# A four-pass FFN beside attention on one core: fillers for TensorE in the setup, the product kept in PSUM, and the score maximum ahead of the residual

## The chip, the cores and the metric

One of the eight cores of a Trainium2 chip runs the whole program. The metric is the device time of one launch in microseconds (us); smaller is better. Engines: TensorE (PE) multiplies into PSUM; VectorE (DVE), ScalarE (ACT) and GpSimd (POOL) do the rest; SyncE (SP) starts the DMAs. PEld is TensorE's weight load, which overlaps its matmuls.

## The reference, cut to what matters

```python
x = x + xattn(layernorm(x), fside, ctx, ctx)      # B=16 batches of 256 tokens, D=256
x = x + ffn(layernorm(x))
# xattn: 16 heads of 16; q = ln(x)@Wq+bq; keys and values = [fside@Wk+bk ; ctx] (512 rows)
#        softmax(q k^T / 4) v, then @Wp + bp
# ffn:   8 experts, dense; for each expert e (w_gate, w_up: 256x1024; w_down: 1024x256)
h   = silu(t @ w_gate[e]) * (t @ w_up[e])
out = sum_e (h @ w_down[e]) * cw[:, e]    # cw: product of two softmaxes, normalised
```

## The kernel before, in words

Every large operand is split into a high part, rounded for the fast fp32 matmul, and the rest, the low part; a product takes three passes (high*high, high*low, low*high). ACT makes the high part by a copy that rounds, DVE or POOL the low part by a subtraction.

The order of all work is written out by hand, as one loop for each engine over turns b = -2..18 of 32 steps. In turn b the attention of batch b runs, one step for each of its 32 score tiles. `ITEMS` gives each step at most one small job of PE with a reader behind it (`do_misc`: transposes, projections; "kT" and "qq" bring keys and queries into `KTs` and `QTs`). From step 19 of turn 2 (`START` = 83) one FFN step f goes with each step, 512 of them: a group of two batches takes 64 of them (8 experts by 8 slices of 128 hidden columns). Attention ends with turn 15; some 85 FFN steps follow without it.

In one joint step PE issues, in this order: `gate(f+1)` (6 matmuls of 512 columns into `ps_g`), `up(f+1)` (6 into `ps_u`), `down(f)` (6 into `ps_o`), every fourth step the 32 small value matmuls ("AV", L735 and L737), the job of the step, one score matmul S (L753) for eight steps ahead, and one T (L763), the transposed score tile that ACT exponentiates into `Pt`. `ps_g` and `ps_u` are the second banks of `ps_s` and `ps_t`, so once the FFN runs S has a single bank and waits until DVE has taken the maximum of the S before (`wait_scores_read`). Before `START` S has two banks, and there is no FFN work.

The FFN step on the other engines, by line:

- ACT `tanh_of` L777: `hf` = tanh(`ps_g`/2), then DVE `gate_of` L937: `hf` = (`hf`+1)*`ps_g`, then DVE `hidden_of` L944: `hf` = `hf`*`ps_u` (the product), then ACT `high_of` L782: `h_hi` from `hf`, then DVE `low_of` L949: `h_lo` = `hf` - `h_hi`, then PE `down`. There is one `hf`, so the next tanh waits for `low_of` (`hl_done`), and `up(f)` waits for the product f-1 (`hf_done`).
- DVE's queue in a step: `gate_of`, `hidden_of`, layernorm statistics, `avs`/`ATT` (end of an octet of steps), `low_of`, `router_weights` (steps 19 to 22, tiny tiles), `Pt_lo` L1077 (the residual of the exponentials of the step before, odd steps only; POOL has the even ones), the job's reader, `normalise`, and last the score maximum `negmax` L1141.
- ACT's: tanh, weight copies, `high_of`, jobs, exp L916. POOL's: low parts of the weights L1172, `Pt_lo` L1237, the output sum L1191.

The setup (turns -2 and -1) loads the projection weights, transposes and projects batch 0, and stacks its keys (`kstack`) and queries.

Of the kernel before, what the change touches and what calls it, by code (L numbers as in the profile page):

```python
# [29 lines left out]
P = 128  # L30
# [6 lines left out]
def bass_xattn_moe_ffn_kernel(nc, x, ctx1, ctx2, Wq, bq, Wk, bk, Wv, bv, Wp, bp, w_router, w_gating,  # L37
# [28 lines left out]
    FC = 2  # L66
# [23 lines left out]
    with ExitStack() as ctx:  # L90
# [306 lines left out]
        def by_dve(i):  # L397
            return i % OCT in DVE_LOW
# [140 lines left out]
        def _(pe):  # L539
# [4 lines left out]
            def project(ps, col, width, a, t, w):  # L544
# [6 lines left out]
                        n += 1  # L551
                return mm

            def transpose_in(ps, src):
                for c in range(DC):
                    for t in range(QT):
                        mm = pe.transpose(ps[:, c * N + t * P:c * N + (t + 1) * P],  # L557
                                          src[:, t, c * P:(c + 1) * P], ident[:])
                return mm
# [116 lines left out]
            def up(f):  # L676

                unit = f // FC
                if f % FC == 0:
                    pe.wait_ge(wl_done, 3 * unit + 2)  # L680
                wait_for(pe, hf_done, f)
                times_tokens(ps_u, f, W[unit % 2]["u"]).then_inc(u_ps, 1)

            def down(f):
# [22 lines left out]

            def body(turn):
                for step in range(STEPS):
                    f = turn.f(step)  # L710
                    if f == 0:
                        before_ffn()
                    if f is not None:
                        if f + 1 < FSTEPS:
                            gate(f + 1)
                            up(f + 1)
                        down(f)

                    d, first = item_at(step, -BEHIND - 1)
                    for i in range(first, first + 4) if turn.has(d) and first % 4 == 0 else ():  # L720
                        h, qt, o = i // QT, i % QT, i // OCT
                        octet = (turn.b + d) * NOCT + o
                        if i == first:
                            turn.wait(pe, lo_dve, d, low_parts(i + 4, True))
                            turn.wait(pe, lo_pool, d, low_parts(i + 4, False))
                        if i % OCT == 0:
                            turn.wait(pe, v_3, d, o + 1)
                            for count in (avs_done, rsum_done):
                                wait_for(pe, count.sem, octet_before(octet) + 1)
                        a = octet_bank(octet)[:, (i % OCT) * VW:(i % OCT + 1) * VW]  # L730
                        for kc in range(KC):
                            slot = (i // 4 * KC + kc) % RING
                            col = (h % 2) * N + qt * P
                            hi = Pt[slot][:].bitcast(BF16)
                            pe.matmul(a, hi[:, 2 * col + 1:2 * (col + P):2], VS[:, kc, h, :],  # L735
                                      start=(kc == 0), stop=False)
                            mm = pe.matmul(a, Pt_lo[slot][:, col:col + P], VS[:, kc, h, :],  # L737
                                           start=False, stop=(kc == KC - 1))
                        mm.then_inc(av_ps.sem, 1)

                    name, k, d, one, freed = misc(turn, step)
                    if name:
                        do_misc(turn, name, k, d, one, freed)

                    d, i = item_at(step, AHEAD)
                    if turn.has(d):
                        h, qt = i // QT, i % QT
                        if i % 4 == 0:
                            turn.wait(pe, kT_done, d, h // 2 + 1)
                            turn.wait(pe, qT_done, d, 2 * (h // 2) + 2)  # L750
                        j = (turn.b + d) * STEPS + i
                        wait_scores_read(pe, j)
                        pe.matmul(score_bank(j)[:], QTs[:, h // 2 % QRING, h % 2, qt * P:(qt + 1) * P],  # L753
                                  KTs[:, h // 2, :], start=True, stop=True).then_inc(s_ps.sem, 1)

                    if turn.has(0):
                        i = step
                        pair, kc = i // KC, i % KC
                        if kc == 0:
                            turn.wait(pe, qm_done, 0, 2 * pair + 2)  # L760
                        j = turn.b * STEPS + i
                        wait_keys_read(pe, j)
                        pe.matmul(key_bank(j)[:], KTs[:, pair, kc * P:(kc + 1) * P],  # L763
                                  QTs[:, pair % QRING].rearrange("p h n -> p (h n)"),
                                  start=True, stop=True).then_inc(t_ps.sem, 1)
# [5 lines left out]
        def _(act):  # L771

            def tanh_of(f):

                act.wait_ge(g_ps, f + 1)
                wait_for(act, hl_done, f)
                act.activation(hf[:], ps_g[:], ACT.Tanh, scale=0.5).then_inc(tanh_done, 1)  # L777

            def high_of(f):

                act.wait_ge(hf_done, f + 1)
                act.activation(h_hi[f % FC][:], hf[:], ACT.Copy).then_inc(hh_done, 1)  # L782

            def weights_high(n, unit):

# [136 lines left out]
        def _(dve):  # L922
# [17 lines left out]
            def hidden_of(f):  # L940

                dve.wait_ge(gate_done, f + 1)
                dve.wait_ge(u_ps, f + 1)
                dve.tensor_tensor(hf[:], hf[:], ps_u[:], ALU.mult).then_inc(hf_done, 1)  # L944

            def low_of(f):

                dve.wait_ge(hh_done, f + 1)
                dve.tensor_tensor(h_lo[f % FC][:], hf[:], h_hi[f % FC][:].bitcast(F32), ALU.subtract).then_inc(hl_done, 1)  # L949

            def weigh_output(f, c):

# [73 lines left out]
            def body(turn):  # L1026
                for step in range(STEPS):
# [41 lines left out]
                        low_of(f + 1)  # L1069
                    if f is not None and f % EXPERT == EXPERT - 1:  # L1070
                        weigh_output(f, 1)
                    router_weights(turn, step)
                    d, i = item_at(step, -1)
                    if turn.has(d) and by_dve(i):
                        turn.wait(dve, exp_done, d, i + 1)
                        slot = i % RING
                        dve.tensor_tensor(Pt_lo[slot][:], Pt[slot][:], Pt[slot][:].bitcast(BF16)[:, 1::2],  # L1077
                                          ALU.subtract).then_inc(lo_dve.sem, 1)
                    name, k, d, one, _ = misc(turn, step)
                    ps = bank(one) if name else None  # L1080
                    if name in ("xT", "cT", "aT", "x2T"):
# [55 lines left out]
                    if turn.has(d):  # L1137
                        turn.wait(dve, s_ps, d, i + 1)
                        if i % 4 == 0:
                            turn.wait(dve, mq_l, d, i // 4 - 1)  # L1140
                        dve.tensor_reduce(negmax[:, (i // 4) % 2, i % 4:i % 4 + 1], score_bank((turn.b + d) * STEPS + i)[:], AX.X, ALU.max,  # L1141
                                          negate=True).then_inc(max_done.sem, 1)

            turns(body)

# [153 lines left out]
```

## Time and profile before

| what | us |
|---|---|
| median of 3 runs | 2788.32 (2787.05 to 2789.99) |
| the profiled execution, its own time | 2787.18 |
| its span on the core | 2785.0 |
| PE busy | 2719.2 (98%) |
| DVE busy | 2198.7 (79%) |
| POOL busy | 1807.1 (65%) |
| ACT busy | 1695.8 (61%) |
| mean granted TensorE clock | 0.994 |

The span is the time between the first and last instruction; some 2.2 us of the launch lie around it. Matmuls are pipelined: a 512-column matmul shows 0.39 us but one starts about every 0.23 us at full clock, so starts tell more than busy shares. The granted clock is a share of 2.4 GHz, and has two levels here, 1.0 and 0.5; ahead of 12.0 us the profile holds no clock record, and a window there reads 1.00 whatever the clock was.

### The profile page before, as it was taken

The page shows a single profiled execution, that of the slowest core. Times are in us where ns is not written, and L with a number is a line of the kernel's source. Part 1 is how long each engine was busy: PE and PEld are TensorE (multiplying, and loading weights), DVE is VectorE, ACT ScalarE, POOL GpSimd, SP SyncE. Part 2 cuts the span into 40 slices and gives each one's busy share as a digit, 9 for nine tenths or more (in the row PEclk, how much of TensorE's full clock was granted, in tenths as well). Part 3 has the DMA queues.
Part 4 walks back from the last instruction along what each step waited for, and adds up shares of the span by engine and source line. Part 5 has one row for each costly group of instructions (what it writes and reads, how often), then busy time and mean ns, then how long its engine had stood idle before and what let it go on. Part 6 is the DMA issues. An engine that isn't in the chain of part 4 may idle for free.

```text
span 2785.0 us, 47540 instructions
## 1 busy us (share of the span) xinstructions
PE 2719.2 (98%) x16416; PEld 2224.1 (80%) x16416; DVE 2198.7 (79%) x3254; ACT 1695.8 (61%) x3241; POOL 1807.1 (65%) x1886
## 2 busy tenths in 40 slices
PE   7789999999999999999999999999999999999998
PEld 5578878888888888878788787887878888888887
DVE  7977788878888788787787888878888878766665
ACT  7866566665666666566666666656666666644443
POOL 6766666666666667666676666766666666654554
PEclk8999999999999999999999999999999999999999
DMA  2113233332333323333232322323323233333332
GB/s 69 39 57 99 80 92 96 91 103 79 96 92 95 99 81 91 95 95 99 79 93 88 103 89 86 99 82 109 95 73 100 76 103 92 95 106 114 106 104 82
DMA packets 251275, 252.27 MB, mean 91 GB/s; under 512 B 15904, under 2 KB 242848, under 8 KB 251040
## 3 DMA queue, kind: packets, MB, share of 16 engines
q1 hardware_dynamic: 251040, 249.25, 29.9%
q8 instruction: 134, 2.20, 0.3%
q14 instruction: 101, 0.83, 0.1%
HBM read 240.66 MB, written 8.52 MB: 89 GB/s over the span
## 4 chain that ended last, share of the span: by engine, by line
PE 87%; DVE 6%; issue 3%; ACT 3%; POOL 1%; DMA 0%; POOLq 0%; ACTq 0%; DVEq 0%
PE ps_s L660 23%; PE ps_t L660 23%; PE ps_o L694 23%; PE ps_s L753 4%; PE ps_t L763 3%; PE ps_m L549 3%; PE ps_a L735 2%; PE ps_a L737 2%; DVE negmax L1141 1%; DVE h_lo L949 1%; DVE Pt_lo L1077 1%; PE ps_m L597 1%; PE ps_m L557 1%; DVE hf L944 1%; ACT h_hi L782 1%
## 5 line engine op out<-in xcount | busy, mean ns | idle before, releaser
L949 DVE TENSOR_TENSOR h_lo<-hf,h_hi 128x512 fp32r<-128x512 f32 x512 | 514.6, 1005 | 230.8 <-ACT h_hi L782 220.5
L782 ACT ACTIVATE h_hi<-hf 128x512 fp32r<-128x512 f32 x512 | 323.9, 633 | 522.0 <-DVE hf L944 522.0
L937 DVE SCALAR_TENSOR_TENSOR hf<-hf,ps_s 128x512 f32<-128x512 f32 x512 | 349.5, 683 | 268.5 <-ACT hf L777 265.4
L777 ACT ACTIVATE hf<-ps_s 128x512 f32<-128x512 f32 x512 | 306.0, 598 | 306.2 <-PE ps_s L660 200.9
L1172 POOL TENSOR_TENSOR wg_lo<-stage_w,wg_hi 128x512 fp32r<-128x512 f32 x256 | 338.8, 1323 | 223.2 <-ACT wg_hi L789 223.0
L1237 POOL TENSOR_TENSOR Pt_lo<-Pt 128x512 f16<-128x512 f32 x256 | 312.4, 1220 | 152.8 <-ACT Pt L916 152.5
L694 PE MATMUL ps_o<-h_hi,wd_hi 128*128 128x512 f32 x1024 | 399.9, 391 | 0.9 <-DVE h_lo L949 0.9
L694 PE MATMUL ps_o<-h_lo,wd_hi 128*128 128x512 f32 x1024 | 399.9, 391 | 0.0
L694 PE MATMUL ps_o<-h_hi,wd_lo 128*128 128x512 f32 x1024 | 398.6, 389 | 0.0
L1172 POOL TENSOR_TENSOR wd_lo<-stage_w,wd_hi 128x512 fp32r<-128x512 f32 x256 | 332.3, 1298 | 82.2 <-ACT wd_hi L789 82.0
L944 DVE TENSOR_TENSOR hf<-hf,ps_t 128x512 f32<-128x512 f32 x512 | 351.8, 687 | 35.5 <-PE ps_t L660 0.8
L916 ACT ACTIVATE Pt<-ps_t 128x512 f32<-128x512 f32 x512 | 304.2, 595 | 121.2 <-PE ps_t L763 117.2
L1172 POOL TENSOR_TENSOR wu_lo<-stage_w,wu_hi 128x512 fp32r<-128x512 f32 x256 | 366.6, 1432 | 0.0
L1141 DVE TENSOR_REDUCE negmax<-ps_s 128x1 f32<-128x512 f32 x512 | 346.2, 678 | 3.6 <-PE ps_s L753 3.5
L660 PE MATMUL ps_s<-xh,wg_hi 128*128 128x512 f32 x1024 | 323.6, 397 | 3.2 <-issue 3.2
L660 PE MATMUL ps_s<-xl,wg_hi 128*128 128x512 f32 x1024 | 319.4, 393 | 0.0
L660 PE MATMUL ps_s<-xh,wg_lo 128*128 128x512 f32 x1024 | 318.3, 392 | 0.0
L660 PE MATMUL ps_t<-xh,wu_hi 128*128 128x512 f32 x1024 | 318.0, 391 | 0.0
L660 PE MATMUL ps_t<-xh,wu_lo 128*128 128x512 f32 x1024 | 316.8, 391 | 0.0
L660 PE MATMUL ps_t<-xl,wu_hi 128*128 128x512 f32 x1024 | 315.2, 389 | 0.0
L1077 DVE TENSOR_TENSOR Pt_lo<-Pt 128x512 f16<-128x512 f32 x256 | 290.1, 1133 | 5.6 <-ACT Pt L916 5.5
L753 PE MATMUL ps_s<-KTs,QTs 128*128 128x512 f32 x512 | 235.4, 460 | 28.0 <-DVE negmax L1141 25.0
(190 smaller groups left out, 5117.6 us busy)
## 6 DMA issues: line engine op xcount, KB each, us to landing
stage_w<-in_L_ffn_w_gate_dram SPq DMA_DIRECT2D x256, 256.0 KB, 2.8
stage_w<-in_L_ffn_w_up_dram SPq DMA_DIRECT2D x256, 256.0 KB, 3.0
stage_w<-in_L_ffn_w_down_dram SPq DMA_DIRECT2D x256, 256.0 KB, 2.7
cwb<-d_cw SPq DMA_DIRECT2D x64, 256.0 KB, 3.8
X<-in_x_dram SPq DMA_DIRECT2D x32, 256.0 KB, 3.6
C<-in_fside_BxSxS_dram SPq DMA_DIRECT2D x16, 256.0 KB, 3.0
KVM<-in_ctx_dram SPq DMA_DIRECT2D x16, 256.0 KB, 2.7
d_x<-X SPq DMA_DIRECT2D x16, 256.0 KB, 2.4
```

Of the source, the lines that this page charges most:

```text
L660: mm = pe.matmul(ps[:], wt[:, c, q * P:(q + 1) * P], tok[:, c].rearrange("p k n -> p (k n)"), start=(n == 0), stop=(n == 3 * DC - 1))
L694: mm = pe.matmul(ps_o[:, c, :], wt[:, q, c * P:(c + 1) * P], hid[:], start=(at == 0 and n == 0), stop=(at == EXPERT - 1 and n == 2))
L753: pe.matmul(score_bank(j)[:], QTs[:, h // 2 % QRING, h % 2, qt * P:(qt + 1) * P], KTs[:, h // 2, :], start=True, stop=True).then_inc(s_ps. ...
L777: act.activation(hf[:], ps_g[:], ACT.Tanh, scale=0.5).then_inc(tanh_done, 1)
L782: act.activation(h_hi[f % FC][:], hf[:], ACT.Copy).then_inc(hh_done, 1)
L937: dve.scalar_tensor_tensor(out=hf[:], in0=hf[:], scalar=1.0, in1=ps_g[:], op0=ALU.add, op1=ALU.mult).then_inc(gate_done, 1)
L944: dve.tensor_tensor(hf[:], hf[:], ps_u[:], ALU.mult).then_inc(hf_done, 1)
L949: dve.tensor_tensor(h_lo[f % FC][:], hf[:], h_hi[f % FC][:].bitcast(F32), ALU.subtract).then_inc(hl_done, 1)
L1077: dve.tensor_tensor(Pt_lo[slot][:], Pt[slot][:], Pt[slot][:].bitcast(BF16)[:, 1::2], ALU.subtract).then_inc(lo_dve.sem, 1)
L1141: dve.tensor_reduce(negmax[:, (i // 4) % 2, i % 4:i % 4 + 1], score_bank((turn.b + d) * STEPS + i)[:], AX.X, ALU.max, negate=True).then_in ...
L1172: pool.tensor_tensor(lo[:], raw_weights(n), hi[:].bitcast(F32), ALU.subtract).then_inc(wl_done, 1)
L1237: pool.tensor_tensor(Pt_lo[slot][:], Pt[slot][:], Pt[slot][:].bitcast(BF16)[:, 1::2], ALU.subtract).then_inc(lo_pool.sem, 1)
```

## The change

Three edits. (1) PE transposes the identity into `ps_a` at six places of turns -2 and -1: 13, 10, 6, 10, 2 and 8 times. Nobody reads these results. (2) The product goes to `ps_u` in place of `hf`; `high_of` and `low_of` read it there. So tanh(f) waits for product f-1 where it waited for `low_of(f-1)`; `up(f)` waits for `low_of(f-1)` where it waited for product f-1; and `high_of(f)` waits for `down(f-2)`, the reader of its buffer. (3) In DVE's queue `router_weights` and `Pt_lo` move from behind `low_of` to the end of the step, behind the job's reader, `normalise` and `negmax`.

```diff
--- before.py
+++ after.py
@@ -550,6 +550,16 @@
                                        start=(n == 0), stop=(n == last))
                         n += 1
                 return mm
+
+            KEEP_BUSY = {(-2, 0): 13, (-1, 2): 10, (-1, 4): 6, (-1, 19): 10, (-1, 22): 2, (-1, 24): 8}
+
+            def keep_busy(turn, step):
+
+                n = KEEP_BUSY.get((turn.b, step), 0)
+                if turn.b == -2 and n:
+                    pe.wait_ge(ident_done, 2)
+                for _ in range(n):
+                    pe.transpose(ps_a[:, 0:P], ident[:], ident[:])
 
             def transpose_in(ps, src):
                 for c in range(DC):
@@ -678,7 +688,7 @@
                 unit = f // FC
                 if f % FC == 0:
                     pe.wait_ge(wl_done, 3 * unit + 2)
-                wait_for(pe, hf_done, f)
+                wait_for(pe, hl_done, f)
                 times_tokens(ps_u, f, W[unit % 2]["u"]).then_inc(u_ps, 1)
 
             def down(f):
@@ -707,6 +717,7 @@
 
             def body(turn):
                 for step in range(STEPS):
+                    keep_busy(turn, step)
                     f = turn.f(step)
                     if f == 0:
                         before_ffn()
@@ -773,13 +784,14 @@
             def tanh_of(f):
 
                 act.wait_ge(g_ps, f + 1)
-                wait_for(act, hl_done, f)
+                wait_for(act, hf_done, f)
                 act.activation(hf[:], ps_g[:], ACT.Tanh, scale=0.5).then_inc(tanh_done, 1)
 
             def high_of(f):
 
                 act.wait_ge(hf_done, f + 1)
-                act.activation(h_hi[f % FC][:], hf[:], ACT.Copy).then_inc(hh_done, 1)
+                wait_for(act, d_ps, DC * (f - 1))
+                act.activation(h_hi[f % FC][:], ps_u[:], ACT.Copy).then_inc(hh_done, 1)
 
             def weights_high(n, unit):
 
@@ -941,12 +953,12 @@
 
                 dve.wait_ge(gate_done, f + 1)
                 dve.wait_ge(u_ps, f + 1)
-                dve.tensor_tensor(hf[:], hf[:], ps_u[:], ALU.mult).then_inc(hf_done, 1)
+                dve.tensor_tensor(ps_u[:], hf[:], ps_u[:], ALU.mult).then_inc(hf_done, 1)
 
             def low_of(f):
 
                 dve.wait_ge(hh_done, f + 1)
-                dve.tensor_tensor(h_lo[f % FC][:], hf[:], h_hi[f % FC][:].bitcast(F32), ALU.subtract).then_inc(hl_done, 1)
+                dve.tensor_tensor(h_lo[f % FC][:], ps_u[:], h_hi[f % FC][:].bitcast(F32), ALU.subtract).then_inc(hl_done, 1)
 
             def weigh_output(f, c):
 
@@ -1069,13 +1081,6 @@
                         low_of(f + 1)
                     if f is not None and f % EXPERT == EXPERT - 1:
                         weigh_output(f, 1)
-                    router_weights(turn, step)
-                    d, i = item_at(step, -1)
-                    if turn.has(d) and by_dve(i):
-                        turn.wait(dve, exp_done, d, i + 1)
-                        slot = i % RING
-                        dve.tensor_tensor(Pt_lo[slot][:], Pt[slot][:], Pt[slot][:].bitcast(BF16)[:, 1::2],
-                                          ALU.subtract).then_inc(lo_dve.sem, 1)
                     name, k, d, one, _ = misc(turn, step)
                     ps = bank(one) if name else None
                     if name in ("xT", "cT", "aT", "x2T"):
@@ -1141,6 +1146,14 @@
                         dve.tensor_reduce(negmax[:, (i // 4) % 2, i % 4:i % 4 + 1], score_bank((turn.b + d) * STEPS + i)[:], AX.X, ALU.max,
                                           negate=True).then_inc(max_done.sem, 1)
 
+                    router_weights(turn, step)
+                    d, i = item_at(step, -1)
+                    if turn.has(d) and by_dve(i):
+                        turn.wait(dve, exp_done, d, i + 1)
+                        slot = i % RING
+                        dve.tensor_tensor(Pt_lo[slot][:], Pt[slot][:], Pt[slot][:].bitcast(BF16)[:, 1::2],
+                                          ALU.subtract).then_inc(lo_dve.sem, 1)
+
             turns(body)
 
 
```

## Rows read from the trace of the kernel before

**Rows 1.** By stage: PE, PEld, DVE, ACT, POOL busy; clock, DMA share, GB/s
```profile
20.00:33.00 13.00, 11.69 (x50) 8.41 (x49) 10.39 (x20) 9.99 (x24) 6.72 (x15) 0.52 0.08 21
33.00:168.00 135.00, 105.16 (x1097) 78.49 (x1096) 120.85 (x221) 105.76 (x228) 104.81 (x161) 0.95 0.11 35
168.00:2390.00 2222.00, 2205.07 (x13389) 1809.97 (x13390) 1795.25 (x2650) 1376.83 (x2638) 1473.00 (x1525) 1.00 0.31 92
2390.00:2780.00 390.00, 386.12 (x1837) 318.70 (x1835) 262.44 (x340) 191.20 (x337) 214.62 (x168) 1.00 0.34 102
```
**Rows 2.** Waits of PE, 175 to 2770 us: total, times, longest
```profile
PE ps_s L753 <- DVE negmax L1141: 16.3, 12, 1.6
```
**Rows 3.** Groups by line: busy, mean ns | idle before, releaser (first three: 175:2770)
```profile
L949 DVE TENSOR_TENSOR h_lo<-hf,h_hi 128x512 fp32r<-128x512 f32 x511 | 513.9, 1006 | 230.1 <-ACT h_hi L782 219.8
L944 DVE TENSOR_TENSOR hf<-hf,ps_t 128x512 f32<-128x512 f32 x510 | 350.4, 687 | 34.6 <-DVE hf L937 0.6
L777 ACT ACTIVATE hf<-ps_s 128x512 f32<-128x512 f32 x510 | 304.8, 598 | 302.3 <-PE ps_s L660 196.9 <-DVE h_lo L949 104.5
...
L1089 DVE TENSOR_TENSOR xT_lo<-ps_m,xT_hi 128x512 fp32r<-128x512 f32 x27 | 18.7, 691 | 8.9 <-ACT xT_hi L884 7.5
```
**Rows 4.** Timeline of DVE: start, us, instruction [idle <-releaser], steps 19 to 21
```profile
346.16 1.86 DVE L949 TENSOR_TENSOR h_lo<-hf,h_hi 128x512 fp32r<-128x512 f32 x1
...
352.84 1.25 DVE L1006 SCALAR_TENSOR_TENSOR css<-lsum 128x2 f32<-128x2 f32 x1
...
354.09 1.53 DVE L1077 TENSOR_TENSOR Pt_lo<-Pt 128x512 f16<-128x512 f32 x1
355.54 0.68 DVE L1141 TENSOR_REDUCE negmax<-ps_s 128x1 f32<-128x512 f32 x1
356.14 0.67 DVE L937 SCALAR_TENSOR_TENSOR hf<-hf,ps_s 128x512 f32<-128x512 f32 x1
```
**Rows 5.** Timeline of PE, step 21 of the same turn
```profile
354.28 0.39 PE L694 MATMUL ps_o<-h_lo,wd_hi 128*128 128x512 f32 x1
356.27 0.50 PE L753 MATMUL ps_s<-KTs,QTs 128*128 128x512 f32 x1 [1.60 <-DVE negmax L1141]
356.96 0.70 PE L660 MATMUL ps_s<-xh,wg_hi 128*128 128x512 f32 x2
```
**Rows 6.** Timelines of DVE, ACT and PE, one FFN step without attention
```profile
2605.30 0.69 DVE L944 TENSOR_TENSOR hf<-hf,ps_t 128x512 f32<-128x512 f32 x1
2606.69 1.47 DVE L949 TENSOR_TENSOR h_lo<-hf,h_hi 128x512 fp32r<-128x512 f32 x1 [0.70 <-ACT h_hi L782]
...
2606.03 0.63 ACT L782 ACTIVATE h_hi<-hf 128x512 fp32r<-128x512 f32 x1 [0.51 <-DVE hf L944]
...
2607.75 0.62 PE L660 MATMUL ps_t<-xh,wu_hi 128*128 128x512 f32 x2
```
**Rows 7.** Timeline of PE in the setup
```profile
4.29 1.11 PE L557 MATMUL ps_m<-ident,C 128*128 128x128 f32 x4 [4.29 <-DMA C<-in_fside_BxSxS_dram]
6.75 1.12 PE L557 MATMUL ps_o<-ident,XN 128*128 128x128 f32 x4 [1.34 <-DVE XN L1023]
8.64 1.19 PE L549 MATMUL ps_m<-wkv_hi,cT_hi 128*128 128x512 f32 x2 [0.77 <-DVE wkv_lo L931]
...
13.03 0.39 PE L549 MATMUL ps_m<-wq_hi,xT_hi 128*128 128x256 f32 x2
...
16.72 0.51 PE L597 MATMUL ps_o<-ident_r,kstack 128*128 128x128 f32 x4 [2.17 <-POOL kstack L1254]
```
**Rows 8.** Waits, 33 to 168 us: total, times, longest (DVE, then PE)
```profile
DVE Pt_lo L1077 <- ACT Pt L916: 5.1, 5, 1.4
...
PE ps_s L753 <- DVE negmax L1141: 8.4, 9, 1.6
```
**Rows 9.** Timeline of PE, one value group and the score behind it
```profile
60.91 0.20 PE L735 MATMUL ps_o<-VS,Pt 128*128 128x49 bf16 x1 [0.24 <-DVE Pt_lo L1077]
...
62.24 0.47 PE L753 MATMUL ps_s<-KTs,QTs 128*128 128x512 f32 x1
```

## The prediction, made before the changed kernel ran

> **What bounds the kernel now.** I read the busy time by stage first, because the bound differs between stages. From 168 us to the end the clock is full and PE is busy 2205 of 2222 us and 386 of 390 us, while DVE has 1795 of 2222 [rows 1]: PE sets the pace for 94% of the span, and nothing that another engine saves counts unless PE waits for it. So the second view is PE's waits in that stretch: one cause only, S waiting for the score maximum, 12 times, 16.3 us in all [rows 2]. Third, the setup, 33 to 168 us: here PE is busy 105 of 135 us and DVE 121 [rows 1], so DVE comes nearest to being the bound, with PE waiting for it at S in 9 places, 8.4 us [rows 8]. Ahead of that the clock matters: 0.52 of full from 20 to 33 us [rows 1]. Fourth, the timelines of the places where waits lie, which give every size below.
>
> **Edit 3, the score maximum first (joint stage).** The 12 waits of [rows 2] sit in step 21 of turns 4 to 15. PE issues the last `down` matmul at 354.28 and S not before 356.27, although such matmuls otherwise start 0.23 apart [rows 5]. The maximum it waits for starts at 355.54, behind a tiny `router_weights` operation that takes 1.25 us and a `Pt_lo` of 1.53 us [rows 4]. One event costs 1.99 - 0.23 = 1.76 us at S; half of the turns have the output transposes between and wait less, 1.1 us, so I take 16.3 + 12 x 0.2 for the restart of the pipe = 18.7 us, and with 0.1 at the next `gate`, 20 us. With the maximum ahead of both it runs as soon as `low_of` ends (352.8), and S(21) at 354.5 waits for nothing. What is late next: the two operations now stand between the maximum and `gate_of`. L937 started at 356.14 [rows 4]; if DVE's work is merely permuted it starts there again, ends at 356.8, and `gate` of the next step, which would like to start near 355.0, waits 1.8 us for it: the stall would only change its name. It is shorter if DVE's work before it shrinks. That hangs on edit 2.
>
> **Edit 2, the product in PSUM.** What it removes: L949 takes 1006 ns on average although L944, the same form with one PSUM operand, takes 687 [rows 3]; the single ones are 1.86 in step 19 [rows 4] and 1.47 in the tail, against 0.69 undisturbed [rows 6]. The long ones coincide with POOL's operations; L949 reads two SBUF tiles, L944 one. The new `low_of` reads PSUM and one SBUF tile and writes a low part, which is exactly the form of L1089: 691 ns [rows 3]. So `low_of` falls to 0.69, by 0.32 on average and by 1.17 in step 19. The trace does not show DVE writing PSUM. For the product I take L944's 0.69; below, it could gain nothing that I can name (0.6); above, L949's 1.0 is the bound. `high_of` reads PSUM like tanh: 598 ns [rows 3] against 0.63 [rows 6]; nothing. The Trainium skill ("SBUF — State Buffer", on the shared port pair) says that a DVE operation with two SBUF inputs and a GpSimd operation exclude each other for a whole instruction; the split between L949 and L944 agrees, and by that rule the new `low_of` is never long.
> What it adds: `up(f+1)` waits for `low_of(f)`. Behind it on PE stand `down`, S, T, everything. In the tail, where a step is shortest: product starts 2605.30, `h_hi` 2606.03, `low_of` 2606.69 and, at 0.69, ends 2607.38; `up` starts at 2607.75 [rows 6]. 0.37 us of slack, in each of about 82 steps. An attention step is longer by S, T and a job (4.95 against 4.08 us), so its slack is about 1.2. It is missed where DVE comes late to `gate_of`: from the product's start to the end of `low_of` are 2.1 us, while `gate` plus what precedes `up` give only 1.4 after a late `gate_of`. Setting every L949 to 0.69 from the end of its `h_hi` and leaving all else as it was, I find lateness outside steps 19 to 21 of 1.0 us (step 14, 0.09 each), 5.1 (steps 25, 29, 31) and 1.9 (tail); about half of it came from a tanh that waited for a long `low_of` (104.5 us of such waits in all [rows 3]) and goes, since tanh now waits for the product. I keep 4 us, and 1 us for the first FFN step.
> The rest of it is steps 19 to 22, 13 turns. Followed through one turn: `low_of` of step 19 ends 346.8 in place of 348.0, `up` wanted 346.65, waits 0.2; the tanh behind it comes 1.3 earlier, `gate_of` about 1.1 earlier. In step 20 `low_of` ends at 351.1, the maximum 351.7; then the tiny operation and `Pt_lo`, both still exposed to POOL, end near 354.2; `gate_of` ends 354.9, the `gate` wanted 355.3: no wait; the chain then ends its `low_of` at 357.0 against an `up` at 356.65: 0.3. So 0.5 us a turn, 6.5 in all. The sum of the joint stage: -20 + 4 + 1 + 6.5 = -8.5; if DVE comes out of step 20 late by another microsecond it is +4, if the freed POOL is faster too, -13. I take -10.
> `high_of`'s new wait for `down(f-2)` costs nothing: PE has issued that `down` before the `up` which the product needs.
>
> **Edit 1, the fillers.** PE stands idle until 4.29 us and again 5.4 to 6.75, 7.9 to 8.64, 14.6 to 16.72 [rows 7]. A 128-column transpose of this kind takes 1.11/4, starts about 0.23 apart at the low clock (1.2 GHz) and half of it at the high one. Thirteen take 2.8 us and start after the identity, at 1.5: end 4.3 to 4.5, just covering the wait for the DMA. If they and the ten behind them raise the clock before 8.64, the 12 key and value matmuls, which took 13.03 - 8.64 = 4.39 us [rows 7], take 12 x 0.23 = 2.76, and the chain behind them (bias, `kstack` on ACT and POOL, keys at 16.72) moves by 1.6 us. The ten fillers behind the projections (1.1 us) fit the idle 2.2 us, the last ten the wait before the first S. If the clock then stays up in part of 20 to 33 us, where PE was busy 11.7 of 13 us at 0.52 of the clock [rows 1], I take a sixth of it, another 2 us. Sum -3.6, bounds -6 and +3 (the fillers late at low clock, see below).
>
> **Edit 3 in the setup.** The maximum and the low parts of the jobs come sooner; DVE's 5.1 us of waiting for exp at `Pt_lo` [rows 8] can be used by them. Against it: the value matmuls need `Pt_lo` of three steps back, which now ends a DVE step later by 0.6 to 1.2 us. I take 0, bounds -5 and +8.
>
> **The sum.** 2787.18 - 10 - 3.6 = 2773.6 for an execution like the profiled one; the median shown is 1.1 higher, so 2774.5.
>
> **The rivals.**
> Rival A, the slower side: `up`'s new wait bites in every step. Mechanism: the chain product, `h_hi`, `low_of` exceeds its 0.37 of slack in the tail, because a product written to PSUM is slow or `low_of` is still long. Deciding point: chain longer by 0.37. Price with L949's durations as they were: 0.4 us in 50 of the tail's steps (`low_of` ended 2608.16, `up` started 2607.75 [rows 6]) = 20, and 2.5 us a turn in steps 19 and 20 = 32, against the 20 saved: +32, less fillers, near 2817. For: writing PSUM from DVE is unseen. Against: reads of PSUM are 0.69 in a thousand rows. 8%.
> Rival B, the fillers do not raise the clock. Ten at the low clock end near 7.5 and push the transposes at 6.75 by 0.7; six more push the key projection from 8.64 to 9.5, and it runs at 0.43 a matmul until a later rise: +1.5 to +3. Time: 2774.5 + 3.6 + 2.5 = 2780.5. For: between 5 and 8.6 us the trace has only transposes, and the clock was still low at 8.64; but only eight of them, with idle time between. 17%. The Trainium skill ("TensorE: Matmul & The Clock Gate", Part 4) states that the full clock does not engage for transposes, which speaks against edit 1; by it the sum would be this one.
> Rival C, the setup turns slower by the late `Pt_lo`. From its end the value group and S take 62.24 + 0.47 - 60.91 = 1.8 us [rows 9], and DVE has only the next maximum and small work, 0.6 to 1.2, to fill it: up to 0.5 us in each of some 20 value groups, 1.1 where the clock is low. +10: 2784.5. 15%.
> Rival D, the stalls only change their name: `gate_of` in step 21 at its old time. Joint stage 0: 2784.5. 12%.
>
> **How the numbers follow.** My forecast 48%, A 8, B 17, C 15, D 12. 0.2% (5.6 us) is about what can be told from no change: below 2782.7 is faster. The forecast and B count as faster, and a fifth of C and D: 0.48 + 0.17 + 0.05 = 0.70; same 0.20, three quarters of C and D; slower 0.10, A and the rest. The likeliest case's own range is 2767 to 2780; with B to D and the unknown costs 2763 to 2787.
>
> **What would show it.** Right: L949 near 690 ns reading `ps_t`; no wait of S for `negmax`; no `hf` tanh waiting for `h_lo`; waits of `up` for `h_lo` under 15 us; clock high by 8.6 us, keys' first transposes near 15.1 in place of 16.72. Wrong: DVE writing PSUM over 0.8 us, waits of `ps_t` L660 in the tail, or turn 0 to 2 longer than before.

## The result, and the profile after

The changed kernel takes 2773.89 us (median of 6, 2771.69 to 2776.83) against 2788.32: ratio 0.9948, 95% interval 0.9936 to 0.9961. The forecast was 2774.5. The profiled execution took 2771.69 us with a span of 2769.6. The total is right; the two parts of the sum are not, and it was luck that their errors had opposite signs.

Rows by stage of the changed kernel, columns as in [rows 1]:

```profile
20.00:33.00 13.00, 10.26 (x47) 7.02 (x45) 9.15 (x18) 10.88 (x26) 8.00 (x16) 0.74 0.13 36
33.00:168.00 135.00, 105.50 (x1090) 78.66 (x1090) 115.12 (x221) 102.59 (x222) 102.43 (x160) 0.93 0.11 33
168.00:2390.00 2222.00, 2218.16 (x13488) 1822.83 (x13489) 1662.21 (x2664) 1383.98 (x2657) 1404.26 (x1537) 1.00 0.30 92
```

(PE, PEld, DVE, ACT and POOL busy; granted clock, DMA share, GB/s.) From 168 to 2390 us DVE has 133 us less to do than in [rows 1] and POOL 69; PE's idle time there fell from 17 to 4 us. In the setup the clock was up for more of 20 to 33 us (0.74 against 0.52) and for a little less of the rest. PE's waits in the joint stage, which were the one line of [rows 2], are now all of another kind (total, times, longest; 160 to 2755 us):

```profile
PE ps_t L670 <- DVE h_lo L961: 2.6, 14, 0.5
```

`up` waits for `low_of`, 14 times; no wait of S is left. The groups that answer to [rows 3] (product, `low_of`, `high_of`, tanh; whole span):

```profile
L794 ACT ACTIVATE h_hi<-ps_t 128x512 fp32r<-128x512 f32 x512 | 306.2, 598 | 451.1 <-DVE ps_t L956 451.1
L961 DVE TENSOR_TENSOR h_lo<-ps_t,h_hi 128x512 fp32r<-128x512 f32 x512 | 353.0, 689 | 213.9 <-ACT h_hi L794 207.6
L788 ACT ACTIVATE hf<-ps_s 128x512 f32<-128x512 f32 x512 | 306.3, 598 | 329.8 <-PE ps_s L670 327.7
...
L956 DVE TENSOR_TENSOR ps_t<-hf,ps_t 128x512 f32<-128x512 f32 x512 | 356.4, 696 | 48.1 <-PE ps_t L670 7.5
```

`low_of` fell from 1006 to 689 ns. The product, now written to PSUM, takes 696 ns against 687. No tanh waits for `h_lo` any more.

To see where the time went I cut each span at two starts: the first gate matmul, and the first matmul of the last `down`. Before they are at 168.59 and 2774.72; after:

```profile
169.20 1.19 PE L670 MATMUL ps_s<-xh,wg_hi 128*128 128x512 f32 x2 [2.71 <-issue]
...
2759.78 0.50 PE L704 MATMUL ps_o<-h_hi,wd_hi 128*128 128x512 f32 x1 [0.85 <-DVE h_lo L961]
```

The setup is 0.6 us longer (forecast: 3.6 shorter). The joint stage, as the stretch between the two cuts is called below, takes 2606.1 us before and 2590.6 after: 15.6 shorter by the unrounded starts (forecast: 10 shorter).

### The profile page after: what moved, and what is told of

The parts are those of the page before. It is cut to its first block, busy times and chain, and to the rows that moved or that the text cites. A ratio compares the mean times of both kernels' runs of the same rounds, so it can differ in the third digit from the quotient of the medians.

```text
span 2769.6 us, 48148 instructions
## 1 busy us (share of the span) xinstructions
PE 2721.2 (98%) x16465; PEld 2228.0 (80%) x16465; DVE 2009.8 (73%) x3254; ACT 1689.5 (61%) x3241; POOL 1720.9 (62%) x1886
## 4 chain that ended last, share of the span: by engine, by line
PE 92%; issue 3%; DVE 2%; ACT 2%; POOL 1%; DMA 0%; SPq 0%; POOLq 0%; ACTq 0%; DVEq 0%
PE ps_t L670 25%; PE ps_o L704 24%; PE ps_s L670 24%; PE ps_s L764 4%; PE ps_t L774 4%; PE ps_m L549 3%; PE ps_a L746 2%; PE ps_a L748 2%; PE ps_m L607 1%; PE ps_m L567 1%; PE ps_m L622 1%; PE ps_m L614 1%; ACT Pt L928 0%; DVE Pt_lo L1154 0%; DVE negmax L1146 0%
## 5 line engine op out<-in xcount | busy, mean ns | idle before, releaser
L794 ACT ACTIVATE h_hi<-ps_t 128x512 fp32r<-128x512 f32 x512 | 306.2, 598 | 451.1 <-DVE ps_t L956 451.1
L961 DVE TENSOR_TENSOR h_lo<-ps_t,h_hi 128x512 fp32r<-128x512 f32 x512 | 353.0, 689 | 213.9 <-ACT h_hi L794 207.6
L1185 POOL TENSOR_TENSOR wg_lo<-stage_w,wg_hi 128x512 fp32r<-128x512 f32 x256 | 337.4, 1318 | 265.5 <-ACT wg_hi L801 264.7
L1250 POOL TENSOR_TENSOR Pt_lo<-Pt 128x512 f16<-128x512 f32 x256 | 289.7, 1132 | 197.9 <-ACT Pt L928 197.0
L956 DVE TENSOR_TENSOR ps_t<-hf,ps_t 128x512 f32<-128x512 f32 x512 | 356.4, 696 | 48.1 <-PE ps_t L670 7.5
L1185 POOL TENSOR_TENSOR wd_lo<-stage_w,wd_hi 128x512 fp32r<-128x512 f32 x256 | 332.1, 1297 | 87.5 <-ACT wd_hi L801 87.5
L1185 POOL TENSOR_TENSOR wu_lo<-stage_w,wu_hi 128x512 fp32r<-128x512 f32 x256 | 332.6, 1299 | 0.0
L1154 DVE TENSOR_TENSOR Pt_lo<-Pt 128x512 f16<-128x512 f32 x256 | 255.3, 997 | 0.7 <-ACT Pt L928 0.7
```

The costliest lines, as they stand in the source:

```text
L794: act.activation(h_hi[f % FC][:], ps_u[:], ACT.Copy).then_inc(hh_done, 1)
L956: dve.tensor_tensor(ps_u[:], hf[:], ps_u[:], ALU.mult).then_inc(hf_done, 1)
L961: dve.tensor_tensor(h_lo[f % FC][:], ps_u[:], h_hi[f % FC][:].bitcast(F32), ALU.subtract).then_inc(hl_done, 1)
L1185: pool.tensor_tensor(lo[:], raw_weights(n), hi[:].bitcast(F32), ALU.subtract).then_inc(wl_done, 1)
L1250: pool.tensor_tensor(Pt_lo[slot][:], Pt[slot][:], Pt[slot][:].bitcast(BF16)[:, 1::2], ALU.subtract).then_inc(lo_pool.sem, 1)
```

## The experiments

Two theories stood after the result. Mine: edits 2 and 3 need each other (the maximum first only renames the stall unless DVE also has less to do), and the fillers' lead is given back because edit 3 delays `Pt_lo` in the setup. The rivals: one of the two carries the gain alone; or the lead goes to later falls of the clock. The table has all runs; "first gate" and "joint stage" are read from each kernel's one profile as above, and "late" means that edit 3 holds from the first FFN step on only.

| kernel | edits | median us | ratio to before, 95% | first gate | joint stage |
|---|---|---|---|---|---|
| before | none | 2788.3 | 1 | 168.6 | 2606.1 |
| after | 1, 2, 3 | 2773.9 | 0.9936 to 0.9961 | 169.2 | 2590.6 |
| fillers_only | 1 | 2785.0 | 0.9979 to 0.9997 | 166.4 | 2609.5 |
| psum_only | 2 | 2775.8 | 0.9939 to 0.9966 | 169.8 | 2593.4 |
| order_only | 3 | 2775.3 | 0.9941 to 0.9966 | 172.9 | 2587.9 |
| no_fillers | 2, 3 | 2777.9 | 0.9950 to 0.9977 | 172.9 | 2590.9 |
| order_joint | 1, 2, 3 late | 2769.7 | 0.9918 to 0.9943 | 167.6 | 2591.0 |
| best | 1, 3 late | 2766.8 | 0.9909 to 0.9934 | 166.7 | 2589.1 |
| wait_only | best + `up`'s wait | 2813.5 | 1.0076 to 1.0103 | 167.4 | 2634.8 |
| best_first13 | best, 13 fillers | 2770.2 | 0.9920 to 0.9945 | 170.4 | 2587.9 |
| best_more | best, 52 more fillers | 2764.7 | 0.9901 to 0.9928 | 164.0 | 2587.9 |
| best_more2 | best_more, 32 more | 2764.3 | 0.9901 to 0.9929 | 163.1 | 2588.0 |

Kernels with the same code in a stage show how far one profile can be trusted. The first gate comes at 168.6 and 169.8 without fillers in the old order (before, `psum_only`), at 166.4, 166.7, 167.4 and 167.6 with the fillers of the change in the old order, and at 172.9 twice without fillers in the new one. The joint stage takes 2590.6 to 2591.0 in the three kernels with edits 2 and 3, and 2587.9 to 2589.1 in the five with edit 3 and not edit 2. So a difference of about 1.2 us between two profiles says nothing.

**Each edit alone.** `fillers_only` is the kernel before with `keep_busy`; `psum_only` with the five lines of `up`, `tanh_of`, `high_of`, `hidden_of` and `low_of`; `order_only` with the block moved.

```diff
+                    keep_busy(turn, step)      # and its table, as in the change; nothing else
```

> The kernel before with edit 1 alone. Theory: transposes of the identity raise the clock (in the changed kernel it rose at 4.7 us, behind 13 of them), the first keys come 1.1 us earlier and the first T 2.0 us earlier, and as DVE bounds turns 0 to 2, most of that lead is kept: the first gate near 167 us in place of 168.6, total 1 to 2.5 us less. Rival: a lead of 2 us is eaten by later drops of the clock and by DVE, the first gate at 168.6 again, total 0. The joint stage (first gate to last down) stays at 2606 us by both.

Measured: first gate 2.2 us earlier. The total is about 3.4 us less, above the 1 to 2.5 of the theory, but the interval of the ratio reaches from 0.8 to 5.9 us. In this profile the joint stage is 3.4 us longer: the clock fell twice for 3.4 us, at 1374.6 and 1715.9 us, each right behind one of the S stalls, which this kernel still has:

```profile
1374.00:1378.00 4.00, 4.00 (x12) 3.12 (x11) 2.87 (x6) 3.06 (x6) 2.58 (x3) 0.57 0.02 4
1715.50:1719.50 4.00, 4.00 (x12) 3.12 (x11) 2.59 (x5) 3.06 (x6) 2.89 (x3) 0.57 0.01 4
```

(columns as in [rows 1]; the clock is the third number from the end). The kernel before has the same 12 stalls, and its clock fell behind none of them in its own profile. So a stall can cost more than its length; how often it does is not known from two profiles. This execution was one of the two slowest of `fillers_only` (2788.28 against a median of 2785.0), so the 3.4 us are no cost of the fillers.

```diff
-                wait_for(pe, hf_done, f)
+                wait_for(pe, hl_done, f)
-                dve.tensor_tensor(hf[:], hf[:], ps_u[:], ALU.mult).then_inc(hf_done, 1)
+                dve.tensor_tensor(ps_u[:], hf[:], ps_u[:], ALU.mult).then_inc(hf_done, 1)
...
```

(with the lines of `tanh_of`, `high_of` and `low_of` that belong to it)

> The kernel before with edit 2 alone. Theory: edits 2 and 3 need each other; with the old order S of step 21 still waits for the maximum behind router_weights and Pt_lo, but DVE comes there up to 1.2 us earlier, so the joint stage loses 6 to 10 of the 15.6 us that the changed kernel saved. Rival 1: edit 2 carries it all, joint stage 15 us shorter, no wait of S left. Rival 2: up's new wait bites without edit 3, joint stage as before or longer. Setup as before (first gate at 168.6) by all.

Measured: joint stage 12.7 us shorter. That is neither the theory's 6 to 10 nor rival 1's 15, but the second half of rival 1 holds, no wait of S is left. The first gate came at 169.8 and not at 168.6: the clock rose at 13.3 us where it rose at 12.0 before, with the same code ahead of it. The wait of PE that remains in the joint stage:

```profile
PE ps_t L660 <- DVE h_lo L950: 4.9, 19, 0.9
```

```diff
-                    router_weights(turn, step)     # behind low_of, with the Pt_lo block under it
...
+                    router_weights(turn, step)     # behind negmax, with the Pt_lo block under it
```

(shortened; the comments are not in the kernel)

> The kernel before with edit 3 alone. Theory: the 12 waits of S for the maximum go and come back as waits of gate for gate_of and of down for low_of, since DVE has no less work: joint stage 0 to 4 us shorter; setup 2 to 4 us longer (the first gate at 171 to 172 us), since Pt_lo, which the value matmuls wait for, ends a maximum later. Total -1 to +3. Rival 1: edit 3 carries the gain, joint stage 12 to 16 us shorter. Rival 2: the setup does not mind the order, first gate at 168.6.

Measured: joint stage 18.2 us shorter, more than with edits 2 and 3 together. Rival 1 is right and my theory of the joint stage falls. The setup is 4.3 us longer than in the kernel before and 3.1 longer than in `psum_only`, which has the same setup; 2 to 4 were expected. The one kind of wait in the joint stage is the one I had predicted, `gate` for `gate_of`, but small:

```profile
PE ps_s L660 <- DVE hf L937: 3.2, 7, 0.5
```

Why it is small is in DVE's timeline. First the lines of the kernel before that [rows 4] leaves out, with POOL's output sum beside them:

```profile
344.05 0.69 DVE L937 SCALAR_TENSOR_TENSOR hf<-hf,ps_s 128x512 f32<-128x512 f32 x1 [2.59 <-ACT hf L777]
344.93 2.54 POOL L1191 TENSOR_TENSOR acc<-acc,wout 128x512 f32<-128x512 f32 x2
348.04 0.91 DVE L1002 TENSOR_TENSOR cprod<-lexp 128x16 f32<-128x16 f32 x1
349.47 0.67 DVE L937 SCALAR_TENSOR_TENSOR hf<-hf,ps_s 128x512 f32<-128x512 f32 x1
```

and the same place in `order_only`:

```profile
348.36 0.69 DVE L937 SCALAR_TENSOR_TENSOR hf<-hf,ps_s 128x512 f32<-128x512 f32 x1 [2.49 <-ACT hf L777]
...
350.46 0.87 DVE L949 TENSOR_TENSOR h_lo<-hf,h_hi 128x512 fp32r<-128x512 f32 x1
351.26 0.68 DVE L1134 TENSOR_REDUCE negmax<-ps_s 128x1 f32<-128x512 f32 x1
...
351.96 0.56 DVE L1002 TENSOR_TENSOR cprod<-lexp 128x16 f32<-128x16 f32 x1
352.44 0.68 DVE L937 SCALAR_TENSOR_TENSOR hf<-hf,ps_s 128x512 f32<-128x512 f32 x1
...
354.81 0.68 DVE L949 TENSOR_TENSOR h_lo<-hf,h_hi 128x512 fp32r<-128x512 f32 x1
355.42 0.68 DVE L1134 TENSOR_REDUCE negmax<-ps_s 128x1 f32<-128x512 f32 x1
356.01 1.24 DVE L1006 SCALAR_TENSOR_TENSOR css<-lsum 128x2 f32<-128x2 f32 x1
...
357.26 1.78 DVE L1142 TENSOR_TENSOR Pt_lo<-Pt 128x512 f16<-128x512 f32 x1
358.96 0.68 DVE L937 SCALAR_TENSOR_TENSOR hf<-hf,ps_s 128x512 f32<-128x512 f32 x1
```

The two `gate_of` at 352.44 and 358.96 stand 6.52 us apart here and 6.67 before (349.47 and 356.14): over that step (20 to 21) the permutation gains next to nothing, as I had said. But the one ahead of them stands only 4.08 us earlier (348.36 to 352.44), where it was 5.42 before (344.05 to 349.47). The 1.34 us are two operations between them, in step 19 to 20: `low_of` takes 0.87 in place of 1.86 ([rows 4]), and `cprod` 0.56 in place of 0.91. The lateness of DVE at the end was inherited from there. The timelines show it in each of the 12 turns that had a stall: `low_of` of step 19 takes 1.85 to 1.87 us before and 0.87 or 0.88 in `order_only`, `cprod` 0.91 and 0.56 or 0.57. (They are turns 3 to 14, counted by the S matmuls; the prediction says 4 to 15.)

The place of this `low_of` in DVE's queue did not change. It starts 2.11 us behind its `gate_of` before and 2.10 in `order_only`, and POOL is in its output sum beside it in both. What differs is where that sum stands: it starts 0.88 us behind `gate_of` before, and 1.13 in `order_only` (at 349.49, 3.00 us for two). So the order of DVE's queue seems to act by way of POOL's timing. Of the 508 `low_of` that the trace of the kernel before has in the joint stage, 224 took more than 0.8 us, and a POOL instruction ran beside each of these; of the 123 beside which POOL was idle nearly throughout, none did. That POOL lengthens them is argued from this; no run took POOL's work away, and why 0.25 us of POOL's timing halve this `low_of` is not shown.

Other operations got shorter too. From 175 to 2390 us, first the kernel before, then `order_only`:

```profile
L949 DVE TENSOR_TENSOR h_lo<-hf,h_hi 128x512 fp32r<-128x512 f32 x420 | 409.5, 975 | 177.1 <-ACT h_hi L782 168.0
...
L1077 DVE TENSOR_TENSOR Pt_lo<-Pt 128x512 f16<-128x512 f32 x209 | 247.0, 1182 | 0.0
L1002 DVE TENSOR_TENSOR cprod<-lexp 128x16 f32<-128x16 f32 x14 | 11.2, 803 | 0.0
```

```profile
L949 DVE TENSOR_TENSOR h_lo<-hf,h_hi 128x512 fp32r<-128x512 f32 x423 | 386.2, 913 | 173.1 <-ACT h_hi L782 164.6
...
L1142 DVE TENSOR_TENSOR Pt_lo<-Pt 128x512 f16<-128x512 f32 x211 | 211.9, 1004 | 0.0
L1002 DVE TENSOR_TENSOR cprod<-lexp 128x16 f32<-128x16 f32 x14 | 7.1, 510 | 0.0
```

DVE has 63 us less of these three kinds (668 to 605) although its trace has a few more records of them. What is left at `gate` is a wait of 0.5 us where I had 1.8.

`no_fillers` is the changed kernel without the call of `keep_busy`:

```diff
-                    keep_busy(turn, step)
```

> The changed kernel without edit 1 (edits 2 and 3 stay). It completes the table of the three edits. Theory: the joint stage is that of the changed kernel (2590.6 us), the first gate is 2.5 to 3.5 us later than its 169.2, so the total is 2776 to 2777.5, as edits 2 or 3 alone (2775.8, 2775.3): of the three edits, 2 and 3 do the same thing and edit 1 adds 2 to 3 us. Rival: without fillers the setup is DVE-bound anyway and nothing is lost: 2774.

Measured: joint stage 2590.9 as the theory had it, first gate 172.9, which is 3.7 us later than in the changed kernel and just over the 3.5 given. With both edits the joint stage is 3 us longer than with edit 3 alone, neither kernel having fillers (2590.9 and 2587.9). The total, 2777.9, is 2 to 2.5 us above edits 2 or 3 alone and just over the range given.

**The order in the setup.** `order_joint` is the changed kernel with the move made conditional (`residuals` holds the moved lines; the comments are not in the kernel):

```diff
+                    if not (f is not None):   # at the old place, behind low_of
+                        residuals(turn, step)   # router_weights and Pt_lo
...
+                    if f is not None:         # at the new place, behind negmax
+                        residuals(turn, step)
```

> The changed kernel, but with Pt_lo and router_weights at their old place in DVE's queue as long as no FFN step runs (up to step 18 of turn 2) and at the new place after. Theory: edit 3 costs the setup what the fillers gained; here the first gate comes near 166.5 us in place of 169.2, the joint stage is as in the changed kernel (2590.6), total 2 to 3 us under the changed kernel. Rival: the setup lost its lead for another reason (later drops of the clock), first gate at 169, total as the changed kernel.

Measured: first gate 1.6 us earlier (2.7 expected), total 2769.65 against 2773.89, 4.2 less where 2 to 3 were expected. The other profiles say the same: against all kernels with an equal setup, the new order puts the first gate 1.6 to 2.8 us later with the fillers and 3.1 to 4.3 without. The waits of PE from 33 to 168 us in `order_only` name the cause:

```profile
PE ps_a L735 <- DVE Pt_lo L1142: 7.9, 10, 1.2
PE ps_s L753 <- DVE negmax L1134: 5.3, 6, 2.2
PE ps_o L735 <- DVE Pt_lo L1142: 3.3, 5, 1.0
```

Value matmuls wait 11.2 us for `Pt_lo`, where before they waited 3.3:

```profile
PE ps_o L735 <- DVE Pt_lo L1077: 2.2, 4, 0.9
PE ps_a L735 <- DVE Pt_lo L1077: 1.1, 3, 0.4
```

In return S waits 3.1 us less for the maximum than in [rows 8].

**Edit 2 on top of edit 3.** `best` leaves the product in `hf`; against `order_joint`:

```diff
-                dve.tensor_tensor(ps_u[:], hf[:], ps_u[:], ALU.mult).then_inc(hf_done, 1)
+                dve.tensor_tensor(hf[:], hf[:], ps_u[:], ALU.mult).then_inc(hf_done, 1)
...
```

> The fillers, and edit 3 from the first FFN step on (the old order before); the product stays in hf as in the kernel before. Theory: edits 2 and 3 remove the same 12 waits, and edit 2 then only adds up's wait for low_of; so without it the joint stage is 2588 us as with edit 3 alone (2587.9), against 2590.6 with both, and with the first gate near 167: 2766 to 2768 in all, 2 to 3 us under the kernel with all three (order_joint, 2769.65). Rival: edit 2 still pays for its shorter low_of when combined, so this one is 1 to 3 us slower than order_joint.

Measured: 2766.78 (2766.13 to 2768.26), joint stage 2589.1 against 2591.0. The intervals of the two ratios overlap, but the profiles bear the theory out: the five joint stages with edit 3 and not edit 2 are all shorter than the three with both (2587.9 to 2589.1 against 2590.6 to 2591.0), by 1.5 to 3.1 us. The 1.2 us by which `best` is the longest of the five stand in one turn, where `gate` waits 1.3 us for `gate_of` in place of at most 0.5. `wait_only` ("the same kernel" in what was expected is `best`) is `best` with one line:

```diff
-                wait_for(pe, hf_done, f)
+                wait_for(pe, hl_done, f)
```

> The same kernel, with one edit: up(f) waits for low_of(f-1) in place of product f-1, though the product stays in hf. That is edit 2's added wait with the long low_of (two SBUF inputs) kept. The theory of the prediction's rival A prices it: in the tail low_of ended 0.4 us behind up's start in 50 steps, 20 us, and up to 2.5 us a turn in steps 19 and 20, less what the new order took: joint stage 20 to 45 us longer than without the wait, total 2790 to 2812. Rival: the chain adapts (a wait of up moves everything behind it, so one lateness absorbs the next) and it costs under 10 us.

Measured: 2813.54, joint stage 45.7 us longer, just over the 20 to 45 expected. PE's waits from 175 to 2790 us are all at `up`:

```profile
PE ps_t L670 <- DVE h_lo L960: 21.4, 67, 0.5
```

Counted from start to start, a step of the tail that waits:

```profile
2640.28 0.61 PE L670 MATMUL ps_s<-xl,wg_hi 128*128 128x512 f32 x2
2641.01 0.73 PE L670 MATMUL ps_t<-xh,wu_hi 128*128 128x512 f32 x2
...
2644.78 0.61 PE L670 MATMUL ps_s<-xl,wg_hi 128*128 128x512 f32 x2
2645.23 0.62 PE L670 MATMUL ps_t<-xh,wu_hi 128*128 128x512 f32 x2
```

0.73 us between the last group of `gate` and `up` where the next step has 0.45. Summed over all steps this distance is 34 us more than in `best`, 16 of them in 39 steps of the tail; the matmuls behind such a wait also start further apart at first, but how the other 12 us divide was not worked out. The prediction's rival A priced this wait at 52 us gross, 20 of them in 50 steps of the tail. So edit 2's shorter `low_of` is what makes its own wait bearable: with the wait and the long `low_of` the kernel is slower than before by 0.9%.

**The fillers.** `best_first13` is `best` with one line changed ("the first kernel" in what was expected of it and of `best_more` is `best`):

```diff
-            KEEP_BUSY = {(-2, 0): 13, (-1, 2): 10, (-1, 4): 6, (-1, 19): 10, (-1, 22): 2, (-1, 24): 8}
+            KEEP_BUSY = {(-2, 0): 13}
```

> The first kernel of this call with the 13 fillers at the start alone; the 36 at the other five places are gone. Theory: the 13 raise the clock by 5 to 8 us, but with idle stretches behind them it falls again before or during the projections, so the first keys come 0 to 0.8 us later than with all, and from 18 to 32 us the clock is low as before: the first gate 1 us later, total +1. Rival: the real transposes and projections keep it up and the 13 do it all, same first gate.

Measured: first gate 3.6 us and total 3.4 us later than `best`, where 1 was expected. PE in the setup, `best_first13`:

```profile
1.53 3.04 PE L562 MATMUL ps_a<-ident 128*128 128x128 f32 x13 [1.53 <-POOL ident L1170]
4.36 1.06 PE L567 MATMUL ps_m<-ident,C 128*128 128x128 f32 x4
6.67 1.11 PE L567 MATMUL ps_o<-ident,XN 128*128 128x128 f32 x4 [1.25 <-DVE XN L1034]
8.99 1.19 PE L549 MATMUL ps_m<-wkv_hi,cT_hi 128*128 128x512 f32 x2 [1.21 <-DVE wkv_lo L942]
9.98 1.05 PE L549 MATMUL ps_m<-wkv_lo,cT_hi 128*128 128x512 f32 x2
```

and the changed kernel:

```profile
1.53 3.04 PE L562 MATMUL ps_a<-ident 128*128 128x128 f32 x13 [1.53 <-POOL ident L1164]
4.78 0.66 PE L567 MATMUL ps_m<-ident,C 128*128 128x128 f32 x4 [0.21 <-DMA C<-in_fside_BxSxS_dram]
5.27 1.25 PE L562 MATMUL ps_a<-ident 128*128 128x128 f32 x10
6.73 0.66 PE L567 MATMUL ps_o<-ident,XN 128*128 128x128 f32 x4 [0.20 <-DVE XN L1035]
7.22 0.82 PE L562 MATMUL ps_a<-ident 128*128 128x128 f32 x6
9.04 0.71 PE L549 MATMUL ps_m<-wkv_hi,cT_hi 128*128 128x512 f32 x2 [1.00 <-DVE wkv_lo L943]
9.58 0.62 PE L549 MATMUL ps_m<-wkv_lo,cT_hi 128*128 128x512 f32 x2
```

Thirteen transposes take 3.04 us at the low clock; ten take 1.25 at the high one. In the changed kernel the first record of the clock, at its full level, is at 4.7 us, and the durations change there: up to then PE had run nothing but transposes. With the 13 alone the first record is at 13.5 us, and the rows at 8.99 and 9.98 still have the low clock's length. So the theory's rise by 5 to 8 us did not come, and the 13 alone bought nothing that shows: their kernel has its first keys at 17.61 us and the first gate at 170.4, `psum_only`, which has no fillers and a rise at 13.3, 17.41 and 169.8. Up to 5.2 us the two kernels run the same instructions, and yet the clock rose in one and not in the other. In the seven kernels with all the fillers the rise lies between 4.5 and 7.5 us, twice ahead of any filler but the 13 (4.5 and 4.7). So the times show that the 36 later fillers are needed for the gain; what they do for the rise itself, and what sets its moment, is open.

`best_more` puts 10 fillers ahead of the aT and 16 ahead of the x2T transposes of turns 1 and 2, into the bank that these overwrite; `best_more2` adds 10 and 6 at steps 30 and 31 of turn -1 and 16 into the gate bank ahead of the first gate. The first of these additions is

```diff
+                if turn.b in (1, 2) and name in ("aT", "x2T"):
+                    for _ in range(10 if name == "aT" else 16):
+                        pe.transpose(ps[:, 0:P], ident[:], ident[:])
```

> The first kernel of this call with 10 fillers ahead of the aT transposes and 16 ahead of the x2T transposes in turns 1 and 2, where PE waits for DVE and the clock fell afterwards (3.4 us low, four times between 100 and 170 us). Theory: DVE bounds these turns, so fewer drops give at most 1 us, and fillers of 1.1 and 1.7 us that are not wholly hidden (the waits are 1.1 to 2.2 us) cost as much: total within 1 us. Rival 1: the drops are what ate the lead of the fillers, first gate 2 us earlier. Rival 2: fillers in front of waited-for work delay it each time, first gate 2 us later.

> The fastest kernel so far (fillers also ahead of aT and x2T in turns 1 and 2, product in hf, late Pt_lo only in the joint stage) with 16 fillers more at the two steps of turn -1 where PE waits for the first maxima (the clock fell at 24.5 us behind them) and 16 into the free gate bank ahead of the first gate, where PE stands 3.5 us and then runs the first 12 to 15 FFN matmuls at the low clock. Theory: the first T 0.5 to 1 us earlier, the first gate and up at the full clock, 1 to 1.5 us: total 1 to 2.5 us less than 2764.65. Rival: what stands between is bound by DVE and ACT, total unchanged or up by 1 where fillers overrun the wait.

Measured: `best_more` 2764.65, 2.1 us less than `best` though the runs of the two overlap, and first gate 2.7 us earlier: rival 1 is right, the fillers pay in turns 1 and 2 also. The clock fell once between 60 and 168 us (at 164.5) in place of three times. `best_more2` has the clock up from 4.5 us on but for one 3.4 us stretch at 110.4, and its first gate is 0.9 us earlier still; its time, 2764.33, can't be told from 2764.65, where the theory had 1 to 2.5 us less. `best_more` and `best_more2` are the fastest kernels of this study.

## Why the prediction was right, and where not

1. **PE bounds the joint stage, so the gain is its waits and no more.** Right. DVE's 133 us less of work brought 15.6.
2. **The 12 stalls of S are worth 20 us and go with the maximum first.** Right: edit 3 alone saved 18.2 us with 3.2 us of waits at `gate` left. The prediction did not see that edit 2 alone removes them too; none is left in any kernel with edit 2 or 3.
3. **A mere permutation of DVE's queue would rename the stall (1.8 us at `gate`; rival D).** Wrong. Edit 3 alone saves 18.2 us. The step that failed is "if DVE's work is merely permuted it starts there again": it took every operation at its old length and DVE as late as before when step 20 begins, and permuted only the last link. In the run the permuted queue reached step 20 some 1.34 us sooner, by a shorter `low_of` and `cprod` in step 19. What remains is a wait of at most 0.5 us, 7 times (3.2 us).
4. **`low_of` at 0.69, the product at 0.69.** Right: 0.689 and 0.696 us.
5. **`up`'s new wait costs 4 + 1 + 6.5 us.** Over-sized. The profile has 2.6 us of idle in 14 waits, 0.5 the longest. Counted from start to start, the distance from `gate` to `up` sums to 6.4 us more than before, 0.7 of them in the first FFN step, where the prediction had 11.5. With 6.4 its sum would have been -13.6 against the measured -15.6; the last 2 us have no experiment. Its slack in the tail held: with `low_of` at 0.69 one step of the tail waits, for 0.2 us. With a long one the tail loses 16 us, near rival A's 20.
6. **The fillers raise the clock by 8.6 us; keys at 15.1.** Mechanism right, size too large: the term was 3.6 us, and `fillers_only` has its first gate 2.2 us earlier. In the changed kernel the clock rose at 4.7 us, the keys' transposes start at 15.60 in place of 16.72, since the key projection began 0.4 us later (9.04 against 8.64; DVE's `wkv_lo` came later). Rival B falls. The Trainium skill ("TensorE: Matmul & The Clock Gate", Part 4) says that the full clock does not engage for transposes; here the full clock came at 4.7 us behind 128-column fp32 transposes alone, and the measurement decides.
7. **Edit 3 costs the setup 0.** Wrong, by 1.6 to 2.8 us with the fillers and 3.1 to 4.3 without. It is rival C's mechanism, the late `Pt_lo`, at less than half of rival C's price of 10. I had balanced it against DVE's 5.1 us of waiting for exp; both terms had rows, and the setup's 0 was a choice between them without one.

So the setup came out 4.2 us above its term and the joint stage 5.6 us below its own, and the two nearly cancelled in the total. That the forecast of 2774.5 lies 0.6 us from the measured time is luck: the terms of edit 1, of `up`'s wait and of edit 3 in the setup were all off. And the prediction had edit 2 as what makes edit 3 pay, where on top of edit 3 it costs 1.5 to 3.1 us. (The last step of the sum is off as well: 2773.6 and the 1.1 us of the median give 2774.7.)

## What to carry to other kernels

A stall at the end of a chain of late operations can be inherited: before saying that a reordering only renames it, follow the chain back to where the engine was last on time, and expect the operations that a busy second engine seems to lengthen to change their length with the order. Two edits that remove the same wait don't add up; try each alone, since the second may only bring its own cost (here `up`'s wait). An order that suits a stage bound by one engine can hurt a stage bound by another, and a condition on the stage gets both.

## What the runs showed of the hardware beyond this

- Writing a DVE product of 128x512 fp32 into PSUM took 696 ns against 687 into SBUF; reading one operand from PSUM in place of SBUF took `low_of` from 1006 to 689 ns. POOL's `wu_lo` (L1172, L1185 after) went from 1432 ns to 1299 with the three edits, to 1341 with edit 2 alone and to 1390 with edit 3 alone.
- With fp32 transposes as fillers the granted clock rose earlier: at 4.7, 5.8, 6.2, 7.0, 7.1, 7.5 and 4.5 us in the seven kernels with all the fillers of the change, at 12.0 to 13.5 us in the five others (one of them with the 13 alone).
- The clock fell in the middle of the joint stage behind two of 12 stalls of PE (at most 1.6 us each) in the profile of `fillers_only`, and behind none of the same 12 in that of the kernel before.
